# First-row unit order, weight steps and low parts in a fused gated cross-attention kernel

## The reference

```
x = x + tanh(g_xattn[0]) * L0_xattn(layernorm(x), ctx)        # 16 heads of 32, no mask
x = x + tanh(g_ffn[0])   * L0_ffn(layernorm(x), w1, conv, w2) # 8-bit activations, ternary weights
x = x + tanh(g_xattn[1]) * L1_xattn(layernorm(x), ctx, mask)  # 8 heads of 64, masked
x = x + tanh(g_ffn[1])   * L1_ffn(layernorm(x), w_gate, w_up, w_down)

# an attention
q = (x @ Wq), k = (ctx @ Wk), v = (ctx @ Wv), split into heads
attn = softmax(where(mask, q @ k.T * scale, -inf));  out = (attn @ v) @ Wo

# L1_ffn: every product's two operands are rounded to fp4 first
def fp4_quant_dequant(x):      # blocks of 16 along the last dimension
    scale = maximum(max(abs(xb)) / 6.0, 1e-12)
    q = GRID[searchsorted(MID, abs(xb / scale))] * sign(xb) * scale
```

## Time and profile before

| | |
|---|---|
| median of 3 runs | 2384.8 us (2383.3 to 2389.01) |
| profiled execution | 2391.48 us, span 2389.7 us, mean granted clock 0.917 |
| TensorE, VectorE, GpSimd, ScalarE busy | 84%, 63%, 51%, 40% of the span |
| DMA | 208.83 MB, 87 GB/s on the mean |
| largest groups | low parts L637: 619.5 us on GpSimd; exponentials L751: 247.8 and their copies L761: 254.0 on ScalarE; maxima L933: 236.0 and L928: 120.1 on VectorE |

### The profile page before, as it was taken

How to read it: one execution, slowest core, us unless ns; L and a number is a source line. 1 busy time by engine, 2 the same in 40 slices (tenths; PEclk the granted TensorE clock), 3 DMA queues, 4 the chain that set the end, 5 groups by cost and what they waited for, 6 DMA issues and landing times. The chain is left out here.

```text
span 2389.7 us, 43091 instructions
## 1 busy us (share of the span) xinstructions
PE 2006.7 (84%) x15208; PEld 1407.2 (59%) x15208; DVE 1503.2 (63%) x2860; ACT 951.2 (40%) x1289; POOL 1213.0 (51%) x1436
## 2 busy tenths in 40 slices
PE   3678998998998579999378898898988986799997
PEld 2456666666666367778245566666665674455553
DVE  3636666666664279887433566666666645789873
ACT  2146656656657573333113333333333352111111
POOL 4037666667657553323211454555554552577763
PEclk8989999999997589999688899999999997899998
DMA  5243443443431231100432344334434342010100
GB/s 173 63 118 92 119 113 95 113 113 96 112 92 34 80 113 32 46 27 28 134 108 80 90 116 134 107 107 129 120 104 120 103 142 70 18 36 31 35 22 31
DMA packets 184026, 208.83 MB, mean 87 GB/s; under 512 B 61480, under 2 KB 145704, under 8 KB 183336
## 3 DMA queue, kind: packets, MB, share of 16 engines
q1 hardware_dynamic: 183848, 206.46, 31.0%
HBM read 138.61 MB, written 67.53 MB: 86 GB/s over the span
## 5 line engine op out<-in xcount | busy, mean ns | idle before, releaser
L637 POOL TENSOR_TENSOR a_p_hl<-a_p,a_p_hl 125x448 bf16<-125x448 f32 x576 | 619.5, 1077 | 689.9 <-ACT a_p_hl L761 659.5
L751 ACT ACTIVATE a_p<-a_psum 125x1344 f32<-125x1344 f32 x192 | 247.8, 1290 | 147.7 <-PE a_psum L1141 140.1
L761 ACT ACTIVATE a_p_hl<-a_p 125x1344 bf16<-125x1344 f32 x192 | 254.0, 1323 | 115.3 <-PE a_psum L1179 112.2
L933 DVE TENSOR_REDUCE a_nm<-a_psum 112x1 f32<-112x750 f32 x256 | 236.0, 929 | 32.9 <-PE a_psum L1161 31.1
L1179 PEld LDWEIGHTS a_psum<-a_v_st,a_p_hl 125*128 125x128 bf16 x4608 | 182.9, 100 | 45.4 <-issue 22.6
L1179 PE MATMUL a_psum<-a_v_st,a_p_hl 125*128 125x65 bf16 (+2 forms) x4608 | 194.4, 197 | 13.9 <-POOL a_p_hl L637 11.6
L1161 PE MATMUL a_psum<-a_k_st,a_q_st 96*112 96x375 bf16 x512 | 136.7, 354 | 75.5 <-DVE a_nm L933 64.8
L1807 PE MATMUL f_conv<-f_u,f_taps 128*128 128x224 f32 x768 | 161.2, 359 | 22.1 <-DVE f_u L1659 21.3
L898 DVE TENSOR_TENSOR a_v_st<-a_psum,a_v_st 125x512 bf16<-125x512 f32 x96 | 66.3, 691 | 160.2 <-ACT a_v_st L729 160.2
L892 DVE TENSOR_TENSOR a_k_tmp<-a_psum,a_k_tmp 128x375 bf16<-128x375 f32 x128 | 69.0, 546 | 151.6 <-ACT a_k_tmp L722 146.6
L1807 PEld LDWEIGHTS f_conv<-f_u,f_taps 128*128 128x128 f32 x768 | 141.6, 191 | 31.6 <-DVE f_u L1659 26.9
(11 more groups left out here) (251 smaller groups left out, 4030.2 us busy)
## 6 DMA issues: line engine op xcount, KB each, us to landing
a_k<-a_k_tmp SPq DMA_DIRECT2D x64, 375.0 KB, 3.0
a_k_st<-a_k SPq DMA_DIRECT2D x96, 187.5 KB, 3.4
kept_k<-a_k SPq DMA_DIRECT2D x96, 187.5 KB, 3.4
a_c<-in_ctx_t SPq DMA_DIRECT2D x16, 750.0 KB, 5.5
ctx_parts<-a_chl SPq DMA_DIRECT2D x16, 750.0 KB, 9.8
a_chl<-ctx_parts SPq DMA_DIRECT2D x16, 750.0 KB, 6.9
a_q_st<-a_q SPq DMA_DIRECT2D x192, 56.0 KB, 2.2
rounded<-a_fw SPq DMA_DIRECT2D x24, 352.0 KB, 3.7
```

The source lines that it names most:

```text
L637: ins = nc.gpsimd.tensor_tensor(p_hl[0:MC, h % 2, 1, cols], p32[0:MC, h % 2, cols], p_hl[0:MC, h % 2, 0, cols], ALU.subtract)
L751: nc.scalar.activation(p32[0:MC, par, :].rearrange("p (b n) -> p b n", b=3), st[0:MC, :, 0:2 * S], ACT.Exp, scale=scale).then_inc(exp_done, 1)
L761: nc.scalar.activation(p_hl[0:MC, par, 0, :], p32[0:MC, par, :], ACT.Copy).then_inc(phi_done, 1)
L933: ins = nc.vector.tensor_reduce(out, sm_[0:HALF, 0:2, 0:MK], AX.XY, ALU.max, negate=True)
```

## The change

1. `prologue_steps` becomes one list that holds the splits of contexts (C) and weights (W) too, in the order in which units need them. Weights arrive in the order Wk, Wq, Wv, Wo, and TensorE waits only for those that a unit uses. Three value units stand ahead of the heads, and the next row's first K, K, Q stand between heads (the table `behind`); only the second maxima unit follows the last head. The loads of the next context are issued at other steps.
2. GpSimd takes the roots of row 1 before it fills the ones rows, and the fill is 16 instructions (8 in a1) of 3 x 1500.
3. `last_unit` goes. In a1 the second maxima unit stands in slot 1 of the next row's first quarter, as it already did in a0.
4. In `weight_step` maxima and inverse stand behind the second maximum of a quarter's first head, the powers behind that of its second; the product is on GpSimd (`scale_weights`), ahead of the low part of the quarter's second head. In a1 the two halves of the normalised row stand at two places, each ahead of the powers.
5. In the last row the low part of odd heads is VectorE's (`low_part`).
6. In f1 the tanh of the gate stands behind the first weight's high part, the first weight's low part ahead of the normalisation, and the wait for the gate behind the low parts.

The diff, cut to its core:

```diff
@@ quarter_units, last_unit, slots_of
-        if q == 0 and b.exists() and b.number != 0 and stacked:
+        if q == 0 and b.exists() and b.number != 0:
             maxima = [("M", 1, b)]
...
-    def last_unit(q, b):
-
-        return [("M", 1, b + 1)] if q == 3 and (b + 1).exists() and not stacked else []
...
-            at = [0, 1, 3, 6, 7][5 - len(units):]
+            at = [0, 1, 2, 3, 6, 7] if len(units) == 6 else [0, 1, 3, 6, 7][5 - len(units):]
@@ prologue_steps
-        steps = [("X", 0, b), ("X", 1, b)]
-        for cc in range(KC):
-            steps += [("K", (cc, 0), b), ("K", (cc, 1), b), ("Q", cc, b)]
+        nb = b + 1
+        steps = [("C", 0, b), ("W", 0, b), ("W", 1, b), ("K", (0, 0), b), ("X", 0, b), ("X", 1, b), ("W", 2, b),
+                 ("K", (1, 0), b), ("Q", 0, b), ("C", 1, b), ("K", (0, 1), b), ("W", 3, b), ("Q", 1, b),
+                 ("K", (1, 1), b), ("V", 0, b), ("V", 1, b), ("K", (2, 0), b), ("K", (2, 1), b), ("Q", 2, b),
+                 ("V", 2, b), ("K", (3, 0), b), ("K", (3, 1), b), ("Q", 3, b), ("C", 0, nb)]
+        if stacked:
+            behind = {1: [("V", 3, b)], 2: [("K", (0, 0), nb)], 3: [("V", 4, b)], 5: [("V", 5, b), ("C", 1, nb)],
+                      7: [("X", 0, nb)], 8: [("X", 1, nb)], 9: [("M", 0, b)], 10: [("K", (0, 1), nb)],
+                      12: [("Q", 0, nb)]}
+        else:
+            behind = {0: [("V", 3, b)], 1: [("V", 4, b)], 2: [("V", 5, b), ("C", 1, nb)], 3: [("K", (0, 0), nb)],
+                      4: [("X", 0, nb)], 5: [("X", 1, nb), ("M", 0, b)], 6: [("K", (0, 1), nb)], 7: [("Q", 0, nb)]}
         for h in range(H):
-            steps += [("heads", h, b)]
-            steps += [("V", j, b) for j in range(NJ) if j * H // NJ == h]
-            if h in (H2, H2 + 1):
-                steps += [("X", h - H2, b + 1)]
-            if h == H2 + 1:
-                steps += [("M", 0, b)]
-        return steps + [("M", 1, b), ("K", (0, 0), b + 1), ("K", (0, 1), b + 1), ("Q", 0, b + 1)]
+            steps += [("heads", h, b)] + behind.get(h, [])
+        return steps + [("M", 1, b)]
@@ SyncE
+        W_ORDER = (1, 0, 2, 3)
+        W_NEEDED = {"K": 1, "Q": 2, "V": 3}
...
+                    if step == ("K", (0, 1), b + 1):
+
+                        sp.wait_ge(w_hi, 4)
+                        sp.wait_ge(w_lo, 4)
                     n = after_unit(step)
-                    if not stacked and step[0] == "V" and step[1] in (NJ // 2 - 1, NJ - 1):
+                    if stacked and step == ("K", (0, 1), b):
+                        load_ctx(b + 1, 0)
+                    if not stacked and step in (("Q", KC - 1, b), ("V", NJ - 1, b)):
 
                         sp.wait_ge(unit_done, n)
-                        load_ctx(b + 1, step[1] * 2 // NJ)
+                        load_ctx(b + 1, 0 if step[0] == "Q" else 1)
@@ GpSimd
             row_roots(Item(0, 0, 0))
-
+            row_roots(Item(1, 1, 1))
+
+            pool.wait_ge(roots, 2)
             pool.wait_ge(preset, 2)
             pool.wait_ge(w_hi, 4)
             pool.wait_ge(w_lo, 4)
-            ones = k_st[m_row:m_row + 3, :, 0:16 * M] if stacked else k_st[m_row:m_row + 3, :, 8 * M:16 * M]
-            nc.gpsimd.memset(ones, 1.0).then_inc(preset, 1)
+            for par in range(2):
+                for c0 in range(0 if stacked else 8 * M, 16 * M, 2 * M):
+                    ins = nc.gpsimd.memset(k_st[m_row:m_row + 3, par, c0:c0 + 2 * M], 1.0)
+                    if (par, c0) != (1, 14 * M):
+                        chain.link(ins)
+            ins.then_inc(preset, 1)
...
+                        if fp4_weights and b.number is None and h == q * HC + 1:
+                            scale_weights(q, b)
+                        if low_by_vector(b, h):
+                            continue
...
+            def scale_weights(q, b):
+
+                pool.wait_ge(f_inverse, b.index * 4 + q - 1)
+                pool.wait_ge(f_rounded, b.index * 4 + q - 1)
+                for n, cols in enumerate(halves):
+                    ins = fp4_rescale(nc.gpsimd, ft[:, cols], fw[:, q % 2, cols],
+                                      f_small[:, cols.start // 16:cols.stop // 16])
+                    if n == 0:
+                        chain.link(ins)
+                ins.then_inc(f_product, 1)
@@ VectorE, weight_step and the last row's low parts
-                step = at - 1 if q == 2 else at
-                if step == 0:
+                if at == 1:
...
-                    link(nc.vector.tensor_scalar(f_small[:, :], f_small[:, :], 1.0 - 2.0 ** -22, None, ALU.mult))
-                if step == 1:
-                    dve.wait_ge(f_rounded, b.index * 4 + q - 1)
-                    link(nc.vector.tensor_tensor(in_blocks(ft[:, :]), in_blocks(w), f_small[:, :].unsqueeze(
-                        2).broadcast_to(blocks), ALU.mult))
-                if step == 2:
+                    nc.vector.tensor_scalar(f_small[:, :], f_small[:, :], 1.0 - 2.0 ** -22, None,
+                                            ALU.mult).then_inc(f_inverse, 1)
+                if at == 3:
+                    dve.wait_ge(f_product, b.index * 4 + q - 1)
                     fp4_powers(link, w, ft[:, :]).then_inc(f_scaled, 1)
+
+            def low_part(b, h):
+
+                hd = b.index * H + h
+                dve.wait_ge(phi_done, hd + 1)
+                dve.wait_ge(pv_done, hd - 1)
+                nc.vector.tensor_tensor(p_hl[0:MC, h % 2, 1, :], p32[0:MC, h % 2, :], p_hl[0:MC, h % 2, 0, :],
+                                        ALU.subtract).then_inc(plo_vector, 1)
...
-                    weight_step(q, b, 2 * j)
...
+                    next_context(2 * j + 1)
                     weight_step(q, b, 2 * j + 1)
-                    next_context(2 * j + 1)
...
-            NORMALISED = {(2, 5): [0], (2, 7): [1]} if stacked else {(2, 3): [0, 1]}
+            NORMALISED = {(2, 5): [0], (2, 7): [1]} if stacked else {(2, 2): [0], (2, 3): [1]}
@@ fp4_ffn, VectorE
             x_moments(0)
+            w_lo(0)
             x_normalise(0)
-            dve.wait_ge(gate_ready, 1)
...
-            for n in range(2 * NG):
+            for n in range(1, 2 * NG):
                 w_lo(n)
-                if n == 0:
+                if n == 1:
                     x_scale(0)
```

More of the change, by code:

```diff
@@ L131, in quarter_units @@
             else:
-                units += chunk[:1] + maxima + chunk[1:] if stacked else maxima + chunk
+                units += chunk[:1] + maxima + chunk[1:] if stacked or q == 0 else maxima + chunk
         if (b + 1).exists():
@@ L538, in quarter @@
                     load_residual(b + -1)
-                for unit in quarter_units(q, b) + last_unit(q, b):
+                for unit in quarter_units(q, b):
                     n = after_unit(unit)
@@ L643, in quarter @@
                     round_weights(q, b)
+            halves = [slice(n * FP4_COLS // 2, (n + 1) * FP4_COLS // 2) for n in range(2)] if fp4_weights else []
+            def scale_weights(q, b):
[7 more added lines that the diff above has]
+                ins.then_inc(f_product, 1)
             def round_weights(q, b):
@@ L648, in round_weights @@
                 pool.wait_ge(f_scaled, b.index * 4 + q - 1)
-                halves = [slice(n * FP4_COLS // 2, (n + 1) * FP4_COLS // 2) for n in range(2)]
                 for op in (ALU.add, ALU.subtract):
@@ L708, in unit_hi_part @@
                 kind, k, b = unit
-                if unit[:2] == ("K", (0, 0)) and (b.number == 1 or not stacked and b.number != 0):
-                    split_ctx(b, 1, None)
                 n = units.next()
@@ L877, in unit_lo_part @@
                 kind, k, b = unit
-                if unit[:2] == ("K", (0, 0)) and (b.number == 1 or not stacked and b.number != 0):
-                    split_ctx(b, 1)
                 n = units.next()
```

127 lines of the change are left out of this document (69 added, 58 removed).

## The result

The changed kernel took 2292.6 us (median of 4, 2283.98 to 2296.44) against 2386.8 for the kernel before on the same chip (median of 4): a ratio of 0.9602, 95% interval 0.9569 to 0.9634. That is 4% faster, 94 us, where I had forecast 130 (2254 us). The time lies inside the range (2228 to 2300), near its upper end, and 6 us from where the rival "half the loop" stood (2287).

A forecast was written before the change was run, and what follows sets the result against it. No engine was full, so gain had to come from TensorE's waits, or an engine setting a stage's pace. Terms 32 + 18.5 + 72 + 4 + 1.5 + 2.4 = 130.4 us gave 2254 us against 2384.8, range 2228 to 2300.

The forecast's parts named there:

- half the loop: Rival, second attention's loop: two VectorE waits go but a third is left; 33 us less gain, 2287 us; chance 0.16.
- my own sign: Second attention's loop: the prediction counts as wrong if its rows take over 89 us; 83 to 84 expected.
- the loop's part: Six rows of the second attention's loop: 12 us saved a row, 72 in all, bounds 9 and 13.5 a row.
- First rows: First row of each attention: earlier scores and fewer waits save 32 us in the first, 18.5 in the second.
- The three landmarks of a0: First attention's first row: scores start at 57.5, their stage takes 46.7 us, the tail behind it 3.5.
- (a): Second attention's loop: the normalised row's transposes no longer wait 4.83 us for VectorE; about 2 more from the clock.
- the general gains: Second attention's loop: of 2.8 us other wait a row, 1.4 goes; 1.0 comes as new waits.
- (b): Second attention's loop: the moved second maxima unit loses its 3.31 us wait; products behind it gain 1.5 from the clock.
- GpSimd's product at nothing: Second attention's loop: the rounding's product on GpSimd costs nothing, as GpSimd sat idle there for 6.31 us.
- the port: Rival: each product on GpSimd holds up VectorE, 0.8 us in each of 24 pieces, 19 us; 2273 us; chance 0.10.
- the slower one: Rival: GpSimd's product waits for the inverse, delaying low parts, exponentials and values; 6.5 us a piece, 2410 us; chance 0.04.
- Last rows and f1: Savings of 4 us in the first attention's last row, 1.5 in the second's, 2.4 at the last block's start.

## Why the prediction was right, and where it was wrong

**Direction and range: right, the range in part by luck.** The stages that I named gave the time. TensorE's wait for the transposes was VectorE's order, as the run with the halves alone shows, and so was most of the maxima unit's (3.31 to 1.22 with the unit in its old place). But one term of the loop was wrong by 8 us a row, 48 in all. Alone it would have put the time at 2302, outside the range; terms elsewhere that came out better brought it back in. By my own sign ("The prediction is wrong if the rows take over 89 us") the loop's part is wrong: rows of 89.6 us at a granted clock of 0.95, where I had asked for 83 to 84 and 0.97.

**First rows: right in size, a0's partly for a wrong reason.** The three landmarks of a0 lie within 1 us of the forecast. But I read the 15.8 us stall as roots that stand behind the fill, and priced the roots' move as what removes it. Alone it makes the kernel slower (2401). The fill itself holds the normalisation, and the pieces are what lets it through. The row could not tell the two apart: a wait for roots, which came after the fill, looks the same whether or not the next instruction would have been held too. I had counted the cutting in pieces at nothing; in the changed kernel it is worth 7 us by the medians, 11 us of a0 by the profiles. In a1's first row 5.88 us of wait for queries became 3.07 (2.7 forecast), but a new one of 5.54 stands at that row's end, the same as in the loop.

**(a), the transposes' wait: right.** Forecast 4.83 and a share of the clock; the halves apart gave 5.0 a row, the weight steps with the product 4.2 more. (a) with the general gains was 7.2 a row; measured 9.2, of which 2.1 are the fall of the maxima unit's wait, which I had booked under (b).

**(b), the maxima unit: the step that failed.** "now it stands after the next head's transposed scores, behind work that needs nothing of it. It goes." The wait goes, but I booked it, 3.31, and 1.5 of clock behind it as gain, 4.8 a row. It was -3.2: 8 us a row, 48 in all, of which better terms, in the loop and elsewhere, gave back 19. Two things were not read. First, what else ran during the wait: the queries' way through DRAM. From the query unit's start to the scores that wait it is 10.0 to 12.2 us in every loop row of the changed kernel and of the runs that keep its slots (12.0 to 13.9 where the unit stands a slot earlier). In the kernel before that distance was 12.7 to 12.9, so on the mean some 2 us could be had there, not 4.8. The numbers were in the trace, and I had priced the same way (7.84, 5.88) in the first rows but not in the loop. Second, what the moved unit displaced: a full key unit went behind the waiting scores, which costs 3.4 to 4.2 us a row. With both key units ahead, the unit off the row's end is worth nothing that the medians show (2272.1 and 2271.0). The rival with half the loop spoke of a third wait and had nearly the right time (2287), but named VectorE for it. It was SyncE's chain, so its time was right by luck.

**GpSimd's product at nothing: right**, 0.4 us a row. Both rivals on it, the port and the slower one, are out for this kernel. What two engines do to each other did bear on it, at the fill.

**Last rows and f1: right in sum.** 6.3, 0.7 and 2.8 against 4, 1.5 and 2.4. In a0's last row two exponentials stand 6.1 apart, as said. f1's part was not run alone. At f1's start VectorE's wait is 0.99 instead of 3.40.

**What beats both kernels.** The change without the move of the maxima unit (2271.0), or with it behind both key units (2272.1; 2268.4 with the earlier slots), each about 5% under the kernel before and 1% under the changed one. The three can't be told apart.

## What to carry to other kernels

Before a wait is booked as gain, look at what else runs while it lasts, and above all at transfers on their way: measure the distance from their source to their use, and take only what is left over. When a piece is moved into a slot, price the piece that it pushes out, and on which side of the next wait that lands. When one engine's stall ends with another's long instruction, ask whether the order or the instruction itself holds it: they need different cures.

## What the runs showed of the hardware

A VectorE normalisation of 112 x 512 in f32 (0.50 us an instruction) that started beside a GpSimd memset of 20.09 us ended only with it (20.85 us for two, although its start is recorded 0.02 us ahead of the memset's); beside memsets of 1.4 us one took 1.08 to 1.6 on the mean. Subtractions out of PSUM (0.55 and 0.69 us) and statistics of 112 x 512 (1.42 us for two) beside such a memset were not held.

A set of queries on its way through DRAM, issued by SyncE behind a set of keys, let the scores that wait for it start 3.6 to 3.9 us behind the issue of the queries' reads, and 12.3 to 14.8 us behind the write of the last keys.
